# One-core graph network kernel: ScalarE normalises the rows, tables and constants move, GpSimd zeroes the sums

## The reference

```python
xn = layernorm(x)                                   # mean and variance of each row, no gain, no shift
def gcn(x, W, b):                                   # one graph convolution
    msgs = (x @ W)[src] * edge_weight[:, None]
    return segment_sum(msgs, dst, N) + b
gnn = elu(gcn(elu(gcn(xn, W1, b1)), W2, b2))
# linear attention over all nodes, 8 heads of 32
Q, K, V = elu(xn @ Wq) + 1, elu(xn @ Wk) + 1, xn @ Wv
msg = (Q @ (K.T @ V)) / (Q . K.sum(0) + 1e-6)       # per head
msg = layernorm(msg @ Wm) * g1 + b1
mix = xn + layernorm(relu([xn, msg] @ W1m) @ W2m) * g2 + b2
x = x + gnn + mix
# mixture of experts: 8 experts, top 1, bounded capacity
return x + experts(layernorm(x))
```

## Time and profile before

| | us |
|---|---|
| median of three executions | 5452.69 |
| the profiled execution | 5457.28 |
| its span in the profile | 5455.1 |
| preparation, to the first issue of layer 1 | 147.6 |
| layer 1, to the first issue of layer 2 | 2131.3 |
| layer 2, about | 2319 |
| routing, scattering, experts | 857 |

### The profile page before, as it was taken

One profiled execution on the slowest core, in us unless ns is written; L12 is line 12 of the kernel. 1 busy time (PEld: TensorE's weight loads), 2 busy tenths in 40 slices (PEclk: granted clock), 3 DMA queues, 4 the chain that ended last, 5 costly groups with the idle time before them and its releaser, 6 DMA issues. The chain is left out here.

```text
span 5455.1 us, 91414 instructions
## 1 busy us (share of the span) xinstructions
PE 4213.9 (77%) x25266; PEld 3868.4 (71%) x25267; DVE 2655.7 (49%) x9578; ACT 827.1 (15%) x2507; POOL 3456.1 (63%) x3639
## 2 busy tenths in 40 slices
PE   0577777777777777599888888888888888059998
PEld 0566666666666666588888888888888887048887
DVE  7433333333333333456666666666666665224444
ACT  2001101110111101012222222222222222001111
POOL 0677777777777777577666666666666664532222
PEclk9777777777777777698888888888888888579999
DMA  7444444444444444344444444444444444532121
GB/s 217 135 127 132 131 132 129 132 130 132 129 132 132 130 132 129 94 120 142 135 133 133 135 133 133 135 134 133 134 134 135 134 134 120 156 132 66 67 72 63
DMA packets 409076, 693.82 MB, mean 127 GB/s; under 512 B 108237, under 2 KB 275661, under 8 KB 408893
## 3 DMA queue, kind: packets, MB, share of 16 engines
q0 software_dynamic: 177312, 488.43, 30.9%
q1 hardware_dynamic: 195765, 163.17, 10.0%
q10 hardware_dynamic: 35920, 41.25, 2.2%
HBM read 562.84 MB, written 129.68 MB: 127 GB/s over the span
## 5 line engine op out<-in xcount | busy, mean ns | idle before, releaser
L390 PEld LDWEIGHTS sums<-sel,rows 128*128 128x128 f32 x13312 | 1930.7, 226 | 890.5 <-issue 460.2
L390 PE MATMUL sums<-sel,rows 128*128 128x64 f32 x13312 | 1935.6, 309 | 797.3 <-DVEq L505 427.0
L446 POOL DMA_INDIRECT rows<-h,idx x1664 | 1590.6, 956 | 758.1 <-issue 546.1
L446 POOL DMA_INDIRECT rows<-xn,idx x1664 | 1582.9, 951 | 643.7 <-issue 635.2
L398 DVE TENSOR_SCALAR sel<-cols,rel_now,wgt_now 128x64 f32<-128x64 f32 x3360 | 782.4, 337 | 7.9 <-DVE wgt_now L457 0.2
L404 DVE TENSOR_TENSOR agg<-agg,sums 128x128 f32 x832 | 240.2, 289 | 740.2 <-issue 551.1
L944 PE MATMUL row_ps<-w,hidden 128*128 128x256 f32 x832 | 320.8, 556 | 3.2 <-ACT hidden L1106 3.2
L1805 PE MATMUL y_ps<-w,e_hidden 128*128 128x256 f32 x1248 | 287.1, 390 | 0.0
L1793 PE MATMUL e_hidden_ps<-tokens_t,w 128*128 128x256 f32 x1248 | 280.2, 382 | 4.7 <-DVE e_hidden L1862 3.9
L601 DVE TENSOR_TENSOR pre<-z,b_g 128x256 f32<-128x256 f32 x98 | 41.6, 425 | 492.4 <-PE z L596 492.4
L944 PEld LDWEIGHTS row_ps<-w,hidden 128*128 128x128 f32 x832 | 241.7, 305 | 50.5 <-ACT hidden L1106 3.4
(11 more groups left out here) (211 smaller groups left out, 4667.2 us busy)
## 6 DMA issues: line engine op xcount, KB each, us to landing
xe<-zeros ACTq DMA_DIRECT2D x104, 258.0 KB, 4.1
rows<-xn,idx POOLq DMA_INDIRECT x1664
rows<-h,idx POOLq DMA_INDIRECT x1664
w<-in_ffn_w POOLq DMA_DIRECT2D x16, 1024.0 KB
tile<-xn SPq DMA_DIRECT2D x105, 128.0 KB
ln_rows<-in_x SPq DMA_DIRECT2D x52, 256.0 KB
xn<-ln_normed ACTq DMA_DIRECT2D x52, 256.0 KB, 4.3
kv_tile<-xn SPq DMA_DIRECT2D x104, 128.0 KB, 2.2
```

The source lines that it names most:

```text
L390: last = nc.tensor.matmul(sums[:, g, h, :], rows[:, u, k, h * P:(h + 1) * P], sel[:, u, k, :], start=(c == 0), stop=(c == GROUP - 1))
L446: nc.gpsimd.indirect_dma_start(out=rows[:, u, k, :], out_offset=None, in_=source, in_offset=bass.IndirectOffsetOnAxis(ap=idx[:, u, k:k + 1 ...
```

## The change

- The preparation works on the 98 row tiles that hold nodes (49 blocks instead of 52) with seven slots; the tiles behind them in `xn`, normalised zeros before, are stored as zeros by one transfer at the start.
- VectorE computes mean, variance, reciprocal and a new 128 x 2 value `shift` = -mean / sd. ScalarE normalises: `Identity` with `scale=rstd` and `bias=shift`, two instructions a block, then the store.
- ScalarE's first trip is written out, and a table set is loaded once ahead of it.
- VectorE's first seven blocks stand ahead of the edge reductions, and the tables ahead of the last seven blocks.
- The edge weights are loaded by GpSimd's queue at the start. The other ten constants are loaded at the start of layer 1, between the weights of `keys_values` and those of the dense product; they are scaled at the end of layer 1.
- The first two index tiles of a layer are loaded at the end of the block before it, into a tile `m.idx` that both layers share.
- GpSimd zeroes `agg` for layer 1 inside the preparation. In layer 2 VectorE still does, after the first selection.
- The block `kv` is gone; VectorE does its work at the end of layer 1 (`dve_close`).

```diff
-PSLOTS = 4
+PSLOTS = 7
...
-        n_blocks = NT // PB
+        n_blocks = UNITS // PB
...
+                for u in range(2):
+                    sp.dma_start(m.idx[:, u, :], m.in_src[u]).then_inc(m.idx_first, 16)
+                sp.wait_ge(m.idx_first, 32)
...
+                def normalise(i, s, first):
+                    wait_apart(act, rstd_done, 2 * (i * PSLOTS + s + 1), m.act_passed)
+                    if not first:
+                        act.wait_ge(xn_stored[s], 16 * i)
+                    for j in range(PB):
+                        last = nc.scalar.activation(normed[:, s, j, :], rows[:, s, j, :], ACT.Identity,
+                                                    scale=rstd[:, s, j:j + 1], bias=shift[:, s, j:j + 1])
+                    last.then_inc(xn_done, 1)
                     act.wait_ge(xn_done, i * PSLOTS + s + 1)
                     act.dma_start(...)
...
+                act.preload_act_table_set("sqrt_and_others")
                 act.wait_ge(zero_set, 1)
+                act.dma_start(m.xn[UNITS * P:NP + P, :]..., m.zeros...to_broadcast([P, tiles, D])
+                              ).then_inc(pad_stored, 16)
+                act.wait_ge(eps_set, 1)
+                turn(0, True)
+                with act.Fori(1, loops) as i:
+                    turn(i, False)
...
+                pool.dma_start(m.wgt[:, 0:NCH], m.in_wgt).then_inc(wgt_loaded, 16)
...
+                nc.gpsimd.memset(m.agg[:, :, :], 0.0).then_inc(agg_zeroed, 1)
...
+                def scale(i, s):
+                    dve.wait_ge(sd_done, i * PSLOTS + (s + 1))
+                    nc.vector.reciprocal(rstd[:, s, :], sd[:, s, :]).then_inc(rstd_done, 1)
+                    dve.wait_ge(rstd_done, 2 * (i * PSLOTS + s) + 1)
+                    nc.vector.scalar_tensor_tensor(shift[:, s, :], mv[:, s, :, 0], -1.0, rstd[:, s, :],
+                                                   ALU.mult, ALU.mult).then_inc(rstd_done, 1)
...
                 for u in range(2):
-                    sp.dma_start(idx[:, u, :], m.in_src[u]).then_inc(idx_loaded[u], 16)
                     mix.load(sp, u, u)
...
+                if layer == 1:
+                    for u in range(2):
+                        sp.wait_ge(rows_loaded[u][BANKS - 1], 16 * GROUP * SUB * loops)
+                        sp.dma_start(idx[:, u, :], m.in_src[u]).then_inc(m.idx_first, 16)
...
+                pool.wait_ge(m.idx_first, 32 * layer)
+                turn(0)
+                wait_apart(pool, rows_used[1], 1, m.pool_passed)
+                turn(1)
...
-                nc.vector.memset(m.agg[:, :, :], 0.0).then_inc(agg_zeroed, 1)
+                take(0, 0)
+                if layer == 2:
+                    nc.vector.memset(m.agg[:, :, :], 0.0).then_inc(agg_zeroed, 1)
                 mix.dve_begin(dve)
                 dense.dve_begin(dve)
-                take(0, 0)
...
+        for to, of in consts:
+            sp.dma_start(to, of).then_inc(consts_loaded, 16)
...
+    def dve_close(dve):
+        wait_apart(dve, consts_loaded, 16 * len(consts), m.passed)
+        nc.vector.tensor_scalar(m.ln1_gh[:, :], m.ln1_gh[:, :], -0.5, None, ALU.mult).then_inc(scaled, 1)
...
+        nc.vector.memset(m.kv[:, :, :], 0.0).then_inc(kv_zeroed, 1)
+        wait_apart(dve, total_done, 1, m.passed)
```

More of the change, by code:

```diff
@@ L200, in store, with turn @@
                                   normed[:, s, :, :]).then_inc(xn_stored[s], 16)
-                act.wait_ge(eps_set, 1)
-                with act.Fori(0, loops) as i:
+                def turn(i, first):
                     for s in range(PSLOTS):
@@ L246, in _, with statistics, turn @@
                 nc.vector.memset(m.eps[:, :], LN_EPS).then_inc(eps_set, 1)
+                def statistics(i, s):
+                    dve.wait_ge(x_loaded[s], 16 * i + 16)
+                    for j in range(PB):
+                        last = nc.vector.bn_stats(stats[:, s, j, :], rows[:, s, j, :])
+                    last.then_inc(stats_done, 1)
+                    wait_apart(dve, stats_done, i * PSLOTS + s + 1, m.passed)
+                    for j in range(PB):
+                        last = nc.vector.bn_aggr(mv[:, s, j, :], stats[:, s, j, :])
+                    last.then_inc(mv_done, 1)
+                def scale(i, s):
[4 more added lines that the diff above has]
+                                                   ALU.mult, ALU.mult).then_inc(rstd_done, 1)
+                def turn(i, first):
+                    for s in range(PSLOTS):
+                        statistics(i, s)
+                        if s:
+                            scale(i, s - 1)
+                        elif not first:
+                            scale(i - 1, PSLOTS - 1)
+                turn(0, True)
                 dve.wait_ge(edges_loaded, 32)
@@ L262, in _ @@
                 nc.vector.tensor_tensor(more[:, 1:2], least[:, :], taken[:, :], ALU.is_lt).then_inc(spans_done, 1)
[L263 to L298, removed]
+                with dve.Fori(1, loops - 1) as i:
                     turn(i, False)
-                normalise(loops - 1, PSLOTS - 1, False)
                 dve.wait_ge(iotas_done, 4)
@@ L439, in _, with turn, ready @@
             def _(pool):
[L440 to L449 removed]
+                def turn(u):
+                    for k in range(SLOTS):
+                        nc.gpsimd.indirect_dma_start(
+                            out=rows[:, u, k, :], out_offset=None, in_=source,
+                            in_offset=bass.IndirectOffsetOnAxis(ap=idx[:, u, k:k + 1], axis=0)
+                        ).then_inc(rows_loaded[u][k // (GROUP * SUB)], 16)
+                def ready(i, u):
+                    pool.wait_ge(idx_loaded[u], 16 * i)
+                    wait_apart(pool, rows_used[u], i + 1, m.pool_passed)
+                pool.wait_ge(m.idx_first, 32 * layer)
+                turn(0)
+                wait_apart(pool, rows_used[1], 1, m.pool_passed)
+                turn(1)
+                with pool.Fori(1, loops) as i:
+                    for u in range(2):
+                        ready(i, u)
+                        turn(u)
             @block.vector
@@ L562, in _ @@
                 dense.pe_end(pe)
-        mix.after()
 def dense_first(nc, m, sb, sem, ps, shared):
@@ L1115, in attend @@
     mix.load_weights = lambda sp: None
-    mix.after = lambda: None
+    mix.dve_close = lambda dve: None
     return mix
```

97 lines of the change are left out of this document (48 added, 49 removed).

## The result

The changed kernel takes 5500.38 us (median of four executions, 5496.98 to 5504.04), the kernel before 5452.53 beside it: a ratio of 1.0087 [1.0069, 1.0104]. It is 48 us slower, where 47 faster were forecast. The profiled execution has a span of 5502.5 us, against 5455.1.

The account below looks back on a forecast made before the run. VectorE was taken to bound the preparation, GpSimd's issue rate layer 1, TensorE layer 2. Savings 31.3 + 10.1 + 2.7 + 3.0 = 47.1 us gave 5410 (5406 on the median's scale), range 5392 to 5422.

Parts of the forecast that it names:

- the last one of the sum: After the preparation: the stages follow each other, so nothing later takes back the 47.1 us unless a pace changes.
- rival 4: Layer 2 loses clock: 21 us per hundredth, gain gone from 0.858, 5469 us at 0.85; chance 0.04.
- Preparation: Ends at 116.3 us against 147.6, ScalarE setting the pace at 1.85 us a block; 31.3 us saved.
- The first rows: Start of the preparation: first rows land at 10.8 to 16.6 us, taken as 13.5.
- the pair of activations: ScalarE's two normalising instructions per block in the preparation: 0.50 us for the first, 0.59 for the second.
- the two stalls: ScalarE in the preparation loses about 4.6 us to VectorE's edge reductions and about 2.0 to the tables.
- ScalarE's move: Normalisation in the preparation goes from VectorE, the bound at 2.30 us a block, to ScalarE at 1.85.
- GpSimd's zeroing: In the preparation: at most 30 us, ended by 66 us, hidden if it doesn't hold VectorE up.
- Rival 2: GpSimd's zeroing holds VectorE up while both write SBUF: 25 us lost, 5431 us; chance 0.05.
- Start of layer 1: Earlier indices save 2.4 us, a gap of 1.5 instead of 9.18 before the second batch 7.7: together 10.1.
- Between the layers: The kv block's small instructions run while layer 1's last store lands: 2.7 us saved.
- Start of layer 2: GpSimd's third batch starts about 49.4 us into the block instead of 52.4: 3 us saved, bounds 0 and 10.

Follow-up runs that it names:

- e2: Changed kernel plus 360 never executed VectorE increments in layer 1's branch for rows left over; 5416.07 us, ratio 0.994.
- e5: Changed kernel plus 256 never executed VectorE increments in layer 1's branch for rows left over; 5499.89 us.
- e1: Changed kernel with the edge tables again behind all seven-block trips, so only one VectorE trip is written out; 5411.1 us, ratio 0.993.
- e8: As e1, but VectorE normalises the rows again, its second trip is written out and 64 never executed instructions are added; 5424.93 us, ratio 0.9955.
- e11: Kernel before plus 120 executed VectorE increments ahead of its wait for the constants in the preparation; 5450.2 us.

## Why the prediction was wrong

**The step that failed** is the last one of the sum: "Layer 1, layer 2 and the expert stage follow each other, so nothing later takes the gain back unless a pace changes", and with it, in rival 4, that layer 2's "work is unchanged". The work was unchanged; its place in VectorE's program wasn't. Some 50 instructions more ahead of it, most of them in the preparation, put the loop of layer 2 over a border, and 78.5 us were lost there: -35.3 + 78.5 and 4.2 behind layer 2 are the 47.4 by which the span grew. Rival 4 named the layer and the sign, but gave the clock as its cause: the window stands at 0.87 for 0.88, but over layer 2 (2426 to 4640) the granted clock is 0.87 in `e2`, which has no loss, and 0.88 in `e5`, which has it. So it wasn't the cause. What was needed lay in the programs of the two kernels, 3205 to 3548 against 3256 to 3599, and I had used these for the order of instructions alone.

**The other steps, with the border out of the way** (`e1`, `e2`: 5411 and 5416 against a forecast of 5406):

- Preparation: 116.3 predicted, 123.37 measured. The first rows at 13.13 (13.5) and the pair of activations, 1.09, were right. From the first pair at 15.67 to the last at 118.96 there are 48 blocks; without the two stalls that is 1.98 us a block, not 1.85: 6 of the 7 us. In the trip that is written out a block takes 1.69, in the loop 1.9, and more at its ends (2.06 over a whole trip). The stalls were 5.63 and 2.69 for 4.6 and 2.0; the 2.69 bought nothing, as `e1` starts 2.0 earlier without it.
- ScalarE's move: credited with too much. The 31 us of the preparation were set against a VectorE at 2.30 us a block, its wait for the table load in each trip included. `e8` shows that with the table loaded once, and seven slots, VectorE does a block in 1.88 us, and ScalarE with the store's issue in 1.9 (1.94 and 2.06 over a whole trip). So that part of the gain came with the table load or the slots, which no run tells apart; that the three blocks less and the edge reductions beside the rows gave the rest is argued, not shown. The move itself pays by freeing VectorE of the zeroing's lock (`e1` is 14 us faster than `e8`), and when the stores leave ScalarE. As far as the pace of a block goes, the rule of the Trainium skill that I had weighed ("ScalarE: Activation LUTs", Rules for kernel authors) was nearer to what the runs show than my reading of it.
- GpSimd's zeroing: hidden, 21.13 us. Rival 2 does happen on this chip, as `e8` shows, only not for the instructions that stayed on VectorE: its statistics beside the zeroing kept their 0.74 us a pair (43.79). "SBUF — State Buffer" in the Trainium skill, Who interferes with whom, says that VectorE's instructions in a two-port mode and GpSimd's exclude each other for the whole instruction; the 21.88 us agree, if the normalising instruction runs in such a mode, which no row shows. The run with pieces goes beyond what it states.
- Start of layer 1: gap 1.10 (1.5 taken), TensorE 20.0 us in (17 to 21), first gather 0.8 behind the issue (0.4). Right. But layer 1's gathers span 2091.8 us for 2097.9, 6.1 less where the gap alone gave back 8.1: 2.0 were lost later in the layer.
- Between the layers, from the last gather of one to the first of the next: 33.1 before (2248.3 to 2281.4), 30.1 after; 2.7 forecast, 3.0 measured.
- Start of layer 2: the wait did move from GpSimd's second batch to its third. That starts 49.3 us into the block (49.4 forecast, 52.4 before), but 54.4 in `e1` and 54.3 in `e2`. Layer 2's gathers without the border take 2311.3 and 2312.3 against 2315.6, which looks like the 3.0 forecast; `e11`, whose layer 2 is the kernel's before, takes 2306.9, so a saving of that size is not shown.

## What to carry to other kernels

Where a loop on one engine is longer than one block of 256 instructions, note where its first and last instruction stand in that engine's program before and after any edit ahead of it, even one in another stage: here two blocks were free and a third cost 60 to 101 us of some 5450. The signs are a wait for "issue" at the first operation behind the jump back, once in a trip, and packets on the instruction queue that grow with the trips; never executed instructions ahead of the loop move it and make the test. Before moving work off a full engine, see whether a wait beside it (here a table load in each trip) is what fills it.

## What was not expected of the hardware

- Eight instructions that run once, in a place where VectorE waits anyway, made the kernel 103 us slower (5450.1 to 5553.2).
- A waiting VectorE instruction did not get its turn between GpSimd's 50 back-to-back pieces of about 0.5 us: 23.57 us, longer than against the one piece of 21.13.
- Transfers of the preparation reached 328 GB/s at a busy share of 0.92; 221 at 0.73 had been read as 303 at most.
